# Rotated attention of one layer: the sine products read one half of the partitions and write the other

## The reference, cut to what matters

```
q = (x @ Wqa @ Wqb).reshape(b, s, H, D)
kv = (x @ Wkva @ Wkvb).reshape(b, s, KVH, D, 2)
x1, x2 = (x[..., ::2], x[..., 1::2])          # _rope, on q and on k
r1 = x1 * cos - x2 * sin
r2 = x1 * sin + x2 * cos
scores = einsum('bqhd,bkhd->bhqk', q, k) * scale      # causal, softmax, values, projection
```

## Time and profile before

| what | value |
|---|---|
| runs, us | 2353.28, 2356.72, 2361.72 |
| span of the profiled execution, us | 2348.3 |
| its own time outside the span | not given; the median of the runs is 8.4 us above the span |
| TensorE, busy | 2052.1 us, 87% |
| VectorE, busy | 1544.7 us, 66% |
| ScalarE, busy | 1199.0 us, 51% |
| GpSimd, busy | 825.0 us, 35% |
| rope layer: expert work with hosted batches | about 1200 to 1377 us |
| rope layer: attention | about 1380 to 1631 us |

### The profile page before, as it was taken

How to read it: one execution, slowest core, us unless ns; L and a number is a source line. 1 busy time by engine, 2 the same in 40 slices (tenths; PEclk the granted TensorE clock), 3 DMA queues, 4 the chain that set the end, 5 groups by cost and what they waited for, 6 DMA issues and landing times. The chain is left out here.

```text
span 2348.3 us, 52692 instructions
## 1 busy us (share of the span) xinstructions
PE 2052.1 (87%) x20735; PEld 1381.5 (59%) x20735; DVE 1544.7 (66%) x2742; ACT 1199.0 (51%) x2044; POOL 825.0 (35%) x1272
## 2 busy tenths in 40 slices
PE   6999999999959997998689989997599985479996
PEld 3666666666648995555578966664345543335553
DVE  5777777777743435666354447774688875768884
ACT  3444444444343324665623326655477776447774
POOL 4444444444423432332144414441233322433330
PEclk9999999999969998999789989998699997769998
DMA  5000000000000022444000214441244420134441
GB/s 167 1 1 1 1 1 1 1 1 1 1 6 2 14 46 70 113 113 99 2 4 1 55 29 113 113 112 32 70 100 115 113 61 1 42 80 107 113 109 46
DMA packets 142787, 120.97 MB, mean 52 GB/s; under 512 B 11808, under 2 KB 127408, under 8 KB 142548
## 3 DMA queue, kind: packets, MB, share of 16 engines
q1 hardware_dynamic: 142548, 117.64, 21.1%
HBM read 63.48 MB, written 54.12 MB: 50 GB/s over the span
## 5 line engine op out<-in xcount | busy, mean ns | idle before, releaser
L906 DVE TENSOR_REDUCE l_group_mx<-maxima 128x4 f32<-128x1024 f32 x248 | 304.0, 1226 | 69.0 <-PE maxima L699 67.5
L834 ACT ACTIVATE l_group_pr<-scores 128x1024 f32<-128x1024 f32 x256 | 261.5, 1021 | 71.7 <-PE scores L720 69.1
L2171 POOL TENSOR_TENSOR l_wide_tiles_sum<-l_wide_pr 128x256 f32<-128x256 f32 x256 | 180.7, 727 | 212.4 <-ACT l_wide_pr L2114 212.4
L2142 DVE RECIPROCAL l_wide_rc<-bank 128x256 f32<-128x256 f32 x128 | 223.8, 1749 | 8.4 <-PE bank L2075 7.9
L2114 ACT ACTIVATE l_wide_pr<-scores 128x512 f32<-128x512 f32 x256 | 139.1, 595 | 163.1 <-PE scores L2058 163.1
L2126 DVE TENSOR_REDUCE l_wide_mx<-maxima 128x2 f32<-128x512 f32 x248 | 159.4, 685 | 52.6 <-PE maxima L2038 52.0
L906 DVE TENSOR_REDUCE l_slope_mx<-maxima 128x6 f32<-128x768 f32 x124 | 118.9, 959 | 74.2 <-PE maxima L706 72.7
L2104 ACT ACTIVATE l_wide_qk<-bank 128x512 f32<-128x512 f32 x128 | 76.4, 597 | 175.2 <-PE bank L2025 175.2
L906 DVE TENSOR_REDUCE l_rope_mx<-maxima 128x6 f32<-128x768 f32 x124 | 118.8, 958 | 56.3 <-PE maxima L706 55.4
L834 ACT ACTIVATE l_slope_pr<-scores 128x768 f32<-128x768 f32 x128 | 103.5, 809 | 87.0 <-PE scores L727 86.8
L834 ACT ACTIVATE l_rope_pr<-scores 128x768 f32<-128x768 f32 x128 | 103.7, 811 | 77.0 <-PE scores L727 76.8
(11 more groups left out here) (468 smaller groups left out, 4853.5 us busy)
## 6 DMA issues: line engine op xcount, KB each, us to landing
l_group_st<-stack_dram SPq DMA_DIRECT2D x64, 384.0 KB, 5.5
l_slope_st<-stack_dram SPq DMA_DIRECT2D x32, 384.0 KB, 5.6
l_rope_st<-stack_dram SPq DMA_DIRECT2D x32, 384.0 KB, 5.5
stack_dram<-l_group_parts SPq DMA_DIRECT2D x64, 192.0 KB, 2.3
stack_dram<-l_group_parts SPq DMA_DIRECT2D x64, 128.0 KB, 1.9
stack_dram<-l_slope_parts SPq DMA_DIRECT2D x32, 192.0 KB, 2.4
stack_dram<-l_rope_parts SPq DMA_DIRECT2D x32, 192.0 KB, 2.3
stack_dram<-l_slope_parts SPq DMA_DIRECT2D x32, 128.0 KB, 2.3
```

Of the source, the lines that this page charges most:

```text
L834: act.activation(pr[:, i % AHEAD, :, 0:keys], Tp[:, :, 0:keys], ACT.Exp).then_inc(s["exps"], 1)
L906: dve.tensor_reduce(mx[:, b % 2, :, :, i], max_bank(i, b)[:, :, 0:BLOCKS * keys].rearrange("p z (a k) -> p z a k", k=keys), AX.X, ALU.max, ...
L2142: own.done(dve.reciprocal(rc[:], Ob[i % 2][:, S:2 * S]))
L2171: pool.tensor_tensor(tiles_sum[:, i % 2, z, :], pr[:, i % 2, z, 0:S], pr[:, i % 2, z, S:2 * S], ALU.add).then_inc(s["added"], 1)
```

## The change

The weights with exchanged halves and the "swapped" products go, with their entries in NARROW_BANK, NARROW_ORDER, FIRST and EXPERT_HOST. The qk piece on VectorE now reads the one bank three times: all partitions times cos, then, for each half, the other half of the partitions times sin, written to this half. The bank is released behind the third. The table of sines has its halves exchanged, since it is now read on the partitions of the input. The piece stays in slot 2.

```diff
-            [("score", 0, 0), ("max", 5, 1), ("swapped", 0, 3)],
+            [("score", 0, 0), ("max", 5, 1)],
...
-            [("swapped", 0, 3), ("max", 6, 1)],
+            [("max", 6, 1)],
...
-        "pe": [("norm", 0, 0), ("norm", 0, 1), ("qk", 0, 0), ("swapped", 0, 0), ("qk", 0, 1), ("swapped", 0, 1), ("v", 0, 0), ("v", 0, 1)],
+        "pe": [("norm", 0, 0), ("norm", 0, 1), ("qk", 0, 0), ("qk", 0, 1), ("v", 0, 0), ("v", 0, 1)],
...
-        w = sb("w", [P, 4 if kind == "rope" else 2, C])
+        w = sb("w", [P, 2, C])
...
-                dve.tensor_tensor(by_cos[:], bank[:].rearrange("p (a s) -> p a s", a=2),
-                                  angles[:, 0, :].unsqueeze(1).to_broadcast([P, 2, S]), ALU.mult).then_inc(drained[m], 1)
-            elif what == "swapped":
-                if b == 0:
-                    dve.wait_ge(s["set_act"], 2)
-                wait(dve, s["summed"], b)
-                dve.tensor_tensor(by_sin[:], bank[:].rearrange("p (a s) -> p a s", a=2),
-                                  angles[:, 1, :].unsqueeze(1).to_broadcast([P, 2, S]), ALU.mult).then_inc(drained[m], 1)
+                both = bank[:].rearrange("p (a s) -> p a s", a=2)
+                dve.tensor_tensor(by_cos[:], both, angles[:, 0, :].unsqueeze(1).to_broadcast([P, 2, S]), ALU.mult)
+                for z in range(2):
+                    mine, other = slice(64 * z, 64 * z + 64), slice(64 * (1 - z), 64 * (1 - z) + 64)
+                    ins = dve.tensor_tensor(by_sin[mine], both[other], angles[other, 1, :].unsqueeze(1).to_broadcast([64, 2, S]), ALU.mult)
+                ins.then_inc(drained[m], 1)
...
-                    pool.wait_ge(drained[fill["swapped", b][0]], fill["swapped", b][1])
                     pool.wait_ge(drained[fill["qk", b][0]], fill["qk", b][1])
```

More of the change, by code:

```diff
@@ L251 @@
     "slope": {"norm": 1, "qk": 0, "turnmax": 0, "turn1": 1, "v": 0, "turn0": 0},
-    "rope": {"norm": 1, "qk": 0, "swapped": 1, "turnmax": 0, "turn1": 1, "attn": 1, "v": 0, "project": 1, "turn0": 0},
+    "rope": {"norm": 1, "qk": 0, "turnmax": 0, "turn1": 1, "attn": 1, "v": 0, "project": 1, "turn0": 0},
     "group": {"norm": 0, "qk": 1, "turnmax": 1, "turn1": 0, "reg_scores": 1, "attn": 0, "v": 1, "project": 1, "reg_turn": 0, "turn0": 1, "reg_value": 0},
@@ L453 @@
     "rope": {
-        "pe": {(2, 4): "set0", (2, 5): "set1", (2, 6): "set2", (4, 4): "first", (4, 5): "first", (4, 6): "first", (4, 7): "first",
-               (5, 4): "first", (5, 5): "first", (5, 6): "first", (5, 7): "first"},
+        "pe": {(2, 4): "set0", (2, 5): "set1", (2, 6): "set2", (4, 4): "first", (4, 5): "first", (4, 6): "first",
+               (5, 4): "first", (5, 6): "first", (5, 7): "first"},
         "act": {(2, 4): "set0", (2, 7): "set1", (3, 7): "first", (3, 8): "first", (4, 5): "first", (4, 6): "first", (5, 7): "first",
                 (5, 8): "first"},
-        "dve": {(2, 6): "set0", (3, 4): "stat0", (3, 6): "stat1", (4, 7): "first", (4, 8): "first", (5, 5): "first", (5, 6): "first"},
+        "dve": {(2, 6): "set0", (3, 4): "stat0", (3, 6): "stat1", (4, 7): "first", (5, 5): "first"},
         "pool": {(3, 5): "stat0", (4, 8): "first", (5, 8): "first"},
@@ L544, in narrow_attention @@
                 if (what, i, b) in firsts("pe"):
-                    m = {"qk": 0, "swapped": 1}[what] if kind == "rope" and what in ("qk", "swapped") else b % 2
+                    m = 0 if kind == "rope" and what == "qk" else b % 2
                 count[m] += 1
@@ L549, in bank_of @@
         def bank_of(what, b):
-            early = causal and b < HOSTED and what in ("norm", "qk", "swapped", "v")
+            early = causal and b < HOSTED and what in ("norm", "qk", "v")
             return (Ob if early else Mb)[fill[what, b][0]]
@@ L667, in pe_piece @@
                 ins.then_inc(full[m], 1)
-            elif what in ("qk", "swapped"):
-                if what == "qk" and b == 0:
+            elif what == "qk":
+                if b == 0:
                     pe.wait_ge(s["weights"], 1)
@@ L672, in pe_piece @@
                 for z in range(2):
-                    ins = pe.matmul(bank[:, z * S:(z + 1) * S], w[:, z + (2 if what == "swapped" else 0), :], xnt[:, b % 2, :],
+                    ins = pe.matmul(bank[:, z * S:(z + 1) * S], w[:, z, :], xnt[:, b % 2, :],
                                     start=True, stop=True)
@@ L879, in dve_setup @@
                     q = Ob[0][:, C + v * half:C + (v + 1) * half].rearrange("p (j z i) -> p i z j", z=2, i=4)
-                    for at, which in ((v, 0), (1 - v, 2)):
-                        own.done(dve.tensor_scalar(w[:, which, at * half:(at + 1) * half].rearrange("p (i z j) -> p i z j", i=4, z=2), q,
-                                                   float(D8) ** -0.5, None, ALU.mult))
+                    own.done(dve.tensor_scalar(w[:, 0, v * half:(v + 1) * half].rearrange("p (i z j) -> p i z j", i=4, z=2), q,
+                                               float(D8) ** -0.5, None, ALU.mult))
                     k = Ob[0][:, 2 * C + v * 16:2 * C + (v + 1) * 16].rearrange("p (h i) -> p i h", i=4).unsqueeze(3).to_broadcast([P, 4, 4, 2])
-                    for at, which in ((v, 1), (1 - v, 3)):
-                        to = w[:, which, at * half:(at + 1) * half].rearrange("p (i z h e) -> p z i h e", i=4, z=2, e=2)
-                        for z in range(2):
-                            own.done(dve.tensor_copy(to[:, z], k))
+                    to = w[:, 1, v * half:(v + 1) * half].rearrange("p (i z h e) -> p z i h e", i=4, z=2, e=2)
+                    for z in range(2):
+                        own.done(dve.tensor_copy(to[:, z], k))
                 dve.tensor_copy(wv[:], Ob[0][:, 2 * C + 32:2 * C + 64]).then_inc(s["weights"], 1)
```

5 lines of the change are left out of this document (3 added, 2 removed).

## The result

| kernel | median, us | ratio to before [95% interval] | profiled span, us |
|---|---|---|---|
| before | 2353.33 (11 runs) | | 2348.3 |
| changed | 2364.93 (11 runs) | 1.0038 [1.0023, 1.0053] | 2365.1 |
| changed, a second time | 2367.05 (6 runs) | 1.0063 [1.0043, 1.0084] | 2355.6 |
| before, against itself | 2359.32 (12 runs) | 1.0022 [1.0006, 1.0037] | 2352.9 |

The forecast was no change, 2356.7 us. The changed kernel is slower, by 9 us (ratio 1.0038 on 2353; the two medians lie 11.6 apart) in one comparison and by 15 in the other. The last line bounds how finely this can be read: the very same kernel came out 0.22% (5 us) above itself, so the intervals are too narrow by about that much, and the loss is some 4 to 15 us.

A forecast was written before the change was run, and what follows sets the result against it. The prediction took a DMA round trip, not TensorE, to bound the rope attention. Its terms, -1.5 - 0.6 + 2, summed to 0 within uncertainty: 2356.7 us, no change, range 2350 to 2365 (the forecast's own 2352 to 2361).

The forecast's parts named there:

- What bounds the kernel (the DMA round trip): Rope attention: a DMA round trip, not TensorE, holds the rounds, 11 of them at 14.80 us each.
- Part 1: TensorE, slot 0 of each round: the removed products bring TensorE to M some 0.20 us earlier, counted as 0.
- rival 3: TensorE's clock falls to 1.2 GHz in the rope attention: +1.5 us per round, +18, 2375 us; chance 0.05.
- Part 3: GpSimd's sum L1009 and SyncE's queue: sum 0.88 us later after the cosine, 12 rounds cost 1.0 to 2.6 us, +2 taken.
- Part 2: VectorE, slot 2: cosine and two half products of 0.69 us each take 2.06 us; reduce behind M not delayed.
- Part 4: Expert work of the rope layer: two removed product groups of 0.76 us in hosted batches give -1.5 us.
- Part 5: First two rounds of the rope attention, at half clock: round 0 cancels, round 1 gains, -0.6 us.
- Sum: Whole kernel: -1.5 - 0.6 + 2 = 0 within its uncertainty, on a span of 2348.3 us.
- 1 (TensorE is the bound): Rope attention and expert work: TensorE gives the whole product back, 16.4 us, 2340 us; chance 0.08.
- 2 (GpSimd's delay in full, +0.88 a round): Rope attention: the late sum is paid in each of 12 rounds, +8.5 us in all, 2365 us; chance 0.09.
- 4 (crossing costs double): VectorE: half products crossing partitions take 1.38 us each, trio 3.44, +8 us, 2365 us; chance 0.04.
- Distance to the span: Whole kernel: the 8.4 us by which the median of 2356.72 us lies above the profiled span is kept.

The follow-up runs named there:

- no swap: The changed kernel with one sine product over all 128 partitions, each half on its own, exchange of halves left out: ratio 1.0016, on repeat 1.0022.

## Why the prediction was wrong, point by point

- **What bounds the kernel (the DMA round trip)**: right. The stall at M grew, 12.2 to 14.2 us, and taking TensorE's product away won nothing in the rounds.
- **Part 1 (slot 0)**: right as far as it went: no time won in the rounds. That the product's absence could cost something stood only in rival 3. (The 0.20 us is a slip: 1.77 - 1.51 is 0.26. With that, Part 3's range is 0.6 to 2.3 us instead of 1.0 to 2.6.)
- **Part 2 (VectorE)**: right on the durations. Half products of 688 ns, 0.69 to 0.70 apart; the trio from 1453.64 to 1455.73 is 2.09 us, predicted 2.06. Its "Is the reduce behind M delayed? ... No" was read from one round with a long stall and fails where the stall is short: by 0.7 us at M = 1472.97, 1.1 and 0.7 us over the 12 rounds of the two profiles. How much of that reaches the round isn't shown. On the overlap the runs could say more. With the same starting partitions ("no swap") the second product starts 0.60 after the first, 0.08 before its end; where the start changes, as between the cosine and the sines above, 0.70 after it:

```profile
1493.02 0.68 DVE L914 TENSOR_TENSOR l_rope_by_cos<-bank,l_rope_angles 128x512 f32<-128x512 f32 x1
1493.62 0.68 DVE L915 TENSOR_TENSOR l_rope_by_sin<-bank,l_rope_angles 128x512 f32<-128x512 f32 x1
```

  The Trainium skill (VectorE: DVE Perf Modes, section on two Vector instructions with no wait between them) says that an instruction which starts in another quadrant of partitions than the last is held until the earlier ones have finished. The trace agrees: 0.70 against 0.60 us.
- **Part 3 (GpSimd and the queue)**: right in kind and about right in size. Sum 2.17 us after the cosine (2.12 predicted), the queue waiting 6.3 us for the parts instead of 2.0 and 3.9. The landing is 3.1 us later over the 12 rounds, and the rounds of the kernels with a late sum are longer by 1.2 to 2.8 (+2 taken, range 1.0 to 2.6). The slack of 0.24 us for the low part was that of one round: the queue already waited for L1019 in five rounds of the kernel before, so those had none.
- **Part 4 (hosted batches)**: right, -1.9 against -1.5.
- **Part 5 (the first two rounds)**: this step failed most. It said "In round 0 the two cancel. In round 1 ... about 1.0 is gained and some 0.4 returned by the trio: -0.6". It measured +2.3. It took the clock of the start as given by time, but in the kernels without the second product it comes back 4 to 7 us later than in the two profiles of before, and batch 2 is 1.5 us later. On top come the third product (+0.6) and the late sum (+0.9), and the gain it spoke of is there too, 0.6 of the 1.0: +2.4 by these four, +2.3 measured. That the clock makes the 1.5 is argued from the order between kernels, as said above.
- **The clock in the rounds**: the second step that failed, a term that the sum left out. A fall, once in each profile of the changed kernel, makes one round of 16.60 and of 16.56 us.
- **Sum**: against its terms the start is 2.9 us worse, the rounds 1.9 (+3.9 for +2; the one round with a fall alone is 16.60 us against a mean of 15.03 for the other eleven, +1.6), the hosted batches 0.4 better, and the stretch behind the last M, counted as unchanged, 0.7 better (39.6 and 40.6 against 40.7 and 41.0). With the -0.1 that its terms add up to, that makes +3.6; the two stretches measured +3.5. The ratio of 1.0038 is 9 us: 3.5 are these, 1.2 lie ahead of the layer, and the rest is within the 5 us by which the kernel before differed from itself. How much of it is real stays open.
- **Rivals**: 1 (TensorE is the bound) fell. 2 (GpSimd's delay in full, +0.88 a round) fell: 0.10 to 0.23 came, 0.26 at the landing. 3 (the clock falls) was the nearest, and the sign "a granted clock at 0.5 inside 1415 to 1600" came true; it was priced for a clock that stays down (+18), while it comes back within some 7 us, and fell once in each profile of the changed kernel. The argument against it, that the clock held at a stall of 1.54 us, rested on a TensorE that had the second product in each round. 4 (crossing costs double) fell.
- **Distance to the span**: 8.4 us were kept between the profiled span and the median; the profiled execution of the changed kernel took 2367.11 us for a span of 2365.1, so only 2 of these lie around the span and the rest was the spread of executions.

## What to carry to other kernels

When a product is taken off an engine that stalls once per round, ask first what the engine's clock does. The products removed beside a stall were worthless as time, but the kernels that had them kept the clock up through stalls of up to 1.83 us and had it back 4 us sooner at the start. And a slack read from one round, with a long stall, isn't that of the rounds with a short one: look at the spread of the rounds before counting an overlap as free. Work that moves from an engine into a chain of waits (two products into three, all ahead of one sum) should be followed to the last DMA issue, in the unstalled first rounds as well as in a steady one. And run the kernel before against itself: here it differed by 0.22%, a third to more than half of the effect, and untouched stages of one profile by up to 6 us.

## What the hardware showed unexpectedly

- A VectorE product that reads one half of the partitions and writes the other takes no longer (688 ns for 64x512; 691 for 128x512 in place), and half the partitions save nothing. What it loses is the overlap with its neighbour, 0.10 us.
- TensorE's clock fell to 0.50 after stalls of only 1.5 to 2.2 us, in kernels with one product per batch beside the scores; in those with two it held through stalls of up to 1.83 us. Behind their last product four of these five fell as well, three of them at stalls of 2.11 us and more.
- An unread product can be free in the rounds: with it TensorE is busy 9 us more in 175, and rounds are not longer (15.08 against 15.16 and 15.10).
